# Joining the two attention passes of neighbouring batches on rings of single PSUM banks, in a fused attention, state-space and expert kernel

## The reference

```
qkv    = x @ w_qkv.T + b_qkv                # 16 heads of 16 features
attn   = softmax(q @ k.T / 4)               # 512 x 512 for each head
h      = (attn @ v) @ w_out.T + b_out
h      = concatenate([h, txt], axis=1)      # 589 tokens
u      = layernorm(h);  xp = u @ x_proj.T
delta  = softplus(xp[:, :64] @ dt_proj.T + dt_b)
state  = exp(delta * A) * state + delta * B * u     # 589 steps, 256 features x 16 states
h      = h + sum(state * C) + u * D_skip
h      = h + one_of_14_experts(layernorm(h))
h      = h + causal_attention(layernorm(h))
h      = h + two_of_128_experts(layernorm(h))
```

## Time and profile before

| what | us |
|---|---|
| median of 3 runs | 1209.46 |
| lowest, highest | 1206.95, 1211.32 |
| span of the profiled execution | 1222.6 |
| of it, until the end of the last recurrence | 691 |

### The profile page before, as it was taken

One profiled execution on the slowest core, in us unless ns is written; L12 is line 12 of the kernel. 1 busy time (PEld: TensorE's weight loads), 2 busy tenths in 40 slices (PEclk: granted clock), 3 DMA queues, 4 the chain that ended last, 5 costly groups with the idle time before them and its releaser, 6 DMA issues.

```text
span 1222.6 us, 14392 instructions
## 1 busy us (share of the span) xinstructions
PE 929.1 (76%) x4656; PEld 511.5 (42%) x4657; DVE 763.9 (62%) x1348; ACT 440.4 (36%) x819; POOL 205.3 (17%) x248
## 2 busy tenths in 40 slices
PE   6898989879888688974286529999588887548880
PEld 2323432334323243222253229998356565324440
DVE  4803589996899968999779931111467756732225
ACT  1174138750287501873352203444123331212220
POOL 1000001110011100111000142333000203355550
PEclk9989798976889858796687859999799998769995
DMA  3199206873058730597656436664501400249926
GB/s 100 27 326 330 84 23 160 212 166 100 18 151 206 172 109 1 135 213 159 160 181 211 148 128 192 196 195 149 233 1 46 179 6 14 75 140 398 402 75 253
DMA packets 75259, 185.57 MB, mean 152 GB/s; under 512 B 12010, under 2 KB 48573, under 8 KB 72512
## 3 DMA queue, kind: packets, MB, share of 16 engines
q1 hardware_dynamic: 60800, 148.11, 36.9%
q0 software_dynamic: 14400, 36.71, 13.7%
HBM read 124.88 MB, written 43.69 MB: 138 GB/s over the span
## 4 chain that ended last, share of the span: by engine, by line
PE 35%; DVE 29%; issue 19%; DMA 9%; POOL 3%; ACT 2%; another core or an unknown queue 1%; SPq 1%; POOLq 0%; DVEq 0%; ACTq 0%
DVE hst L1639 8%; PE ps L646 7%; DVE hC L1649 5%; PE ps L1139 5%; DMA bc<-bc_dram 4%; DVE mxn L1588 4%; PE ps L1015 3%; PE ps L623 3%; PE ps L1127 2%; POOL ys_dram L1546 2%; PE ps L1087 2%; DMA yodd<-hC 2%; PE ps L741 2%; DVE Hs L2170 1%; PE ps L633 1%
## 5 line engine op out<-in xcount | busy, mean ns | idle before, releaser
L1588 DVE TENSOR_REDUCE mxn<-ps 128x2 f32<-128x1024 f32 x128 | 150.6, 1220 | 60.3 <-PE ps L646 60.0
L1639 DVE TENSOR_TENSOR_SCAN hst<-dA,dBu 128x1180 f32<-128x1180 f32 x64 | 166.9, 2608 | 3.1 <-ACT dA L1209 2.6
L646 PE MATMUL ps<-Kh,Qh 32*128 32x512 f32 x512 | 122.6, 763 | 25.4 <-DVE mxn L1588 24.6
L1217 ACT ACTIVATE Ph<-ps 128x1024 f32<-128x1024 f32 x128 | 125.2, 1077 | 24.1 <-PE ps L741 23.5
L741 PE MATMUL ps<-Qh,Kh 32*128 32x512 f32 x512 | 111.0, 717 | 5.6 <-ACT Ph L1217 5.4
L1630 DVE TENSOR_TENSOR dBu<-dtu,bc 128x1180 f32<-128x1180 f32 x64 | 88.0, 1380 | 14.7 <-DMA bc<-bc_dram 14.5
L1649 DVE TENSOR_TENSOR hC<-hst,bc 128x1180 f32<-128x1180 f32 x64 | 87.2, 1362 | 9.6 <-DMA yodd<-hC 9.6
L1525 POOL DMA_DIRECT2D yS<-hC x24 | 20.8, 868 | 426.6 <-DVE hC L1649 426.6
L1139 PE MATMUL ps<-ring,xgT 128*64 128x256 f32 x512 | 70.1, 395 | 13.6 <-ACT xgT L1477 9.4
L1906 DVE TENSOR_TENSOR yo<-ps,b2r 128x256 f32<-128x256 f32 x32 | 13.6, 425 | 106.4 <-PE ps L938 106.4
L754 PE MATMUL ps<-Ph,Vh 128*32 128x512 f32 x512 | 73.7, 649 | 7.1 <-ACT OT L1221 4.4
(11 more groups left out here) (263 smaller groups left out, 1443.8 us busy)
## 6 DMA issues: line engine op xcount, KB each, us to landing
bc<-bc_dram SPq DMA_DIRECT2D x64, 590.0 KB, 5.9
ring<-in_we SPq DMA_DIRECT2D x16, 2048.0 KB
W<-in_w SPq DMA_DIRECT2D x46, 512.0 KB, 5.9
yS<-hC POOLq DMA_DIRECT2D x24, 590.0 KB, 7.9
yodd<-hC POOLq DMA_DIRECT2D x24, 590.0 KB, 7.8
xs_dram<-zeros SPq DMA_DIRECT2D x1, 8224.0 KB, 43.8
xg<-xs_dram SPq DMA_DIRECT2D x16, 514.0 KB
ys_dram<-zeros SPq DMA_DIRECT2D x1, 5120.0 KB, 48.3
```

The costliest lines, as they stand in the source:

```text
L646: m = nc.tensor.matmul(ps[:, banks.start + hh % 2, :], Qh[HR * hh:HR * (hh + 1), hg, P * i:P * (i + 1)], Kh[HR * hh:HR * (hh + 1), hg, :], ...
L1217: nc.scalar.activation(Ph[:, n % 2, 2 * g:2 * g + 2, :], ps[:, turned_banks(2 * n + g), :], ACT.Exp, scale=float(HD) ** -0.5).then_inc(act ...
L1588: nc.vector.tensor_reduce(slots32(mxn[:, hg % 2, i, :])[:, 2 * g:2 * g + 2, HD], ps[:, score_banks(b, 2 * (QT * hg + i) + g), :], AX.X, AL ...
L1639: nc.vector.tensor_tensor_scan(hst[:, k % 2, :, :].rearrange("p c t -> p (c t)"), dA[:, k % 2, :, :].rearrange("p c t -> p (c t)"), dBu[:, ...
```

## The change

The order of the first attention and the recurrence is written anew. The first pass of batch b + 1 now runs unit by unit beside the second pass of batch b (`attend_ahead`), six units behind: the second pass of batch `eb` goes with units 10 to 15 of the first pass of `eb` and units 0 to 9 of that of `eb + 1`. The lists are

```diff
+        FIRST_SETS = ((0, 1), (2, 3), (5, 6))
+        A_RING, B_RING = (5, 6, 7), (0, 1, 2)
+        PV, MISC = 3, 4
+        LAG = 6
+        ALONE = NU - LAG
+        TURNED = (2, 3, 0, 1)
+        def score_bank(k):
+            if k < 4 * ALONE:
+                return FIRST_SETS[k // 2 % 3][k % 2]
+            return A_RING[k % 3]
+        def unit_at(eb, n):
+            return (eb, ALONE + n) if n < LAG else (eb + 1, n - LAG)
...
+            def score_head(b, u, h):
+                if i == 0 and h == 0:
+                    pe.wait_ge(act_q, 2 * (HG * b + hg) + 2)
+                if freed_by(k):
+                    pe.wait_ge(dve_max, freed_by(k))
+                return nc.tensor.matmul(ps[:, score_bank(k), :], Qh[HR * h:HR * (h + 1), hg, P * i:P * (i + 1)],
+                                        Kh[HR * h:HR * (h + 1), hg, :], start=True, stop=True)
...
+            def turned_head(b, n, x):
+                h = TURNED[x]
...
+                if k >= len(B_RING):
+                    pe.wait_ge(act_p, k - len(B_RING) + 1)
...
+            def both(b, u, eb, n):
+                for x in range(4):
+                    if u is not None:
+                        score_one(b, u, x)
+                    if n is not None:
+                        turned_head(eb, n, x)
+                if n:
+                    weighted(eb, n - 1)
...
+            def attend_ahead(eb):
+                ab = eb + 1
+                for n in range(NU):
+                    if n == 2:
+                        turn_maxima(eb, 2)
+                    elif n in (4, 8, 12):
+                        project(ab, n // 4 - 1, 0)
+                    elif n in (5, 9, 13):
+                        project(ab, n // 4 - 1, 1)
+                    elif n == 6:
+                        turn_maxima(eb, 3)
+                    elif n in (10, 14):
+                        turn_maxima(ab, n // 4 - 2)
+                    elif eb == 0 and n < 2:
+                        project_v(0, n)
+                    b, u = unit_at(eb, n)
+                    both(b, None if eb == 1 and n < LAG else u, eb, n)
+                weighted(eb, NU - 1)
+
+            def first_chain():
+                project(1, 3, 0)
+                turn_heads(0, range(HG))
+                project(1, 3, 1)
+                both(1, ALONE, 0, None)
+                both(1, ALONE + 1, 0, None)
+                turn_values(0, 0)
+                turn_values(0, 1)
+                both(1, ALONE + 2, 0, None)
+                project_out(0, 0)
+                project_out(0, 1)
+                project_v(1, 0)
+                both(1, ALONE + 3, 0, None)
+                project_v(1, 1)
+                both(1, ALONE + 4, 0, None)
+                turn_tokens(0)
+                both(1, ALONE + 5, 0, None)
+                project_x(0)
+                project_dt(0)
...
@@ DVE
+            def head_maxima(b, u, h):
+                dve.wait_ge(pe_s, k + 1)
+                nc.vector.tensor_reduce(slots32(mxn[:, hg % 2, i, :])[:, h:h + 1, HD], ps[:, score_bank(k):score_bank(k) + 1, :], AX.X, ALU.max,
                                         negate=True).then_inc(dve_max, 1)
...
@@ ACT
-                for g in range(2):
-                    act.wait_ge(pe_st, 2 * k + g + 1)
-                    nc.scalar.activation(Ph[:, n % 2, 2 * g:2 * g + 2, :], ps[:, turned_banks(2 * n + g), :], ACT.Exp, scale=float(HD) ** -0.5).then_inc(act_p, 1)
+                for x in range(4):
+                    act.wait_ge(pe_st, 4 * k + x + 1)
+                    nc.scalar.activation(Ph[:, n % 2, TURNED[x], :], ps[:, B_RING[(4 * k + x) % 3], :], ACT.Exp,
+                                         scale=float(HD) ** -0.5).then_inc(act_p, 1)
```

More of the change, by code:

```diff
@@ L119, in fusion_kernel @@
         dA = eb("dA", [P, 2, KC, LP])
[L120 removed]
+        dBu = eb("dBu", [P, 2, KC, LP])
         hst = eb("hst", [P, 2, KC, LP])
@@ L841, in back_ahead @@
-            def back_ahead(eb, cb):
-                for u in range(NU):
-                    tscores(eb, u)
-                    if u:
-                        weighted(eb, u - 1)
-                weighted(eb, NU - 1)
-                turn_heads(eb, range(HG))
-                for half in range(2):
-                    turn_values(eb, half)
-                for half in range(2):
-                    project_out(eb, half)
-                if eb < NB - 1:
-                    for hg in range(QG):
-                        for which in range(2):
-                            project(eb + 1, hg, which, gap_bank(hg, which))
-                room = low if eb == NB - 1 else tail
-                turn_tokens(eb, room)
-                project_x(eb, room)
-                project_dt(eb, room)
-                if eb == NB - 1:
-                    turn_both(cb)
-                    skip(eb)
+                        at = D * (i - first) + P * c
@@ new lines, in scan_beside_chain @@
+            def scan_beside_chain(cb):
+                eb, ab = cb + 1, cb + 2
+                project(ab, 3, 0)
+                project(ab, 3, 1)
+                turn_heads(eb, range(HG))
+                project_v(ab, 0)
+                project_v(ab, 1)
+                turn_values(eb, 0)
+                turn_values(eb, 1)
+                if cb:
+                    for r in range(len(Y_ROUNDS)):
+                        turn_both(cb - 1, r)
+                project_out(eb, 0)
+                project_out(eb, 1)
+                turn_tokens(eb)
+                project_x(eb)
+                project_dt(eb)
@@ new lines, in scan_beside_attention @@
+            def scan_beside_attention():
+                cb, eb = NB - 2, NB - 1
+                for n in range(NS):
+                    if n == 1:
+                        turn_maxima(eb, 2)
+                    elif n == 2:
+                        turn_maxima(eb, 3)
+                    ahead = remaining(n)
+                    behind = units_ahead(n)
+                    for k in range(max(len(ahead), len(behind))):
+                        both(eb, ahead[k] if k < len(ahead) else None, eb, behind[k] if k < len(behind) else None)
+                    if n == 1:
+                        for r in range(len(Y_ROUNDS)):
+                            turn_both(cb - 1, r)
+                    if n == 9:
+                        weighted(eb, NU - 1)
+                        turn_heads(eb, range(HG))
+                    elif n == 10:
+                        turn_values(eb, 0)
+                        turn_values(eb, 1)
+                    elif n == 11:
+                        project_out(eb, 0)
+                        project_out(eb, 1)
+                    elif n == 13:
+                        turn_tokens(eb)
+                        project_x(eb)
+                    elif n == 14:
+                        project_dt(eb)
```

724 lines of the change are left out of this document (385 added, 339 removed).

## The result

| | median us | lowest to highest |
|---|---|---|
| before, 4 runs | 1210.39 | 1206.95 to 1214.40 |
| changed, 4 runs | 1335.21 | 1314.46 to 1347.85 |

The ratio is 1.093, with a 95% interval of 1.0823 to 1.1037. The forecast was 1272, with 1218 to 1302 as its range. The direction was right, and the median lies 33 us above the range. The profiled span went from 1222.6 to 1331.6 us, +109, where the prediction had +67.

The account below looks back on a forecast made before the run. It took DVE to bound the recurrences and to wait for PE's scores in first passes. +51 us at full clock plus 16 for the clock gave +67 on the span, rounded to 1209.5 + 62 = 1272 us; range 1218 to 1302.

Parts of the forecast that it names:

- The joined step: Four first-pass heads, four second-pass heads and four weighted matmuls, on rings of three banks: 4.0 us at full clock.
- The three joined stretches: First pass of one batch beside second pass of another, for batches 0, 1 and 2: 82 + 80 + 80 us.
- Rival 1: Joined steps: PSUM emptying binds, not the ring; step 2.4 us, total 1183 to 1198 us; chance 0.10.
- Rival 2: Joined steps: PE binds and the ring's wait is hidden; step 3.0 us, total 1212 to 1230; chance 0.17.
- Rival 3: The low clock holds for most of the joined stretches; steps of 6.8 us, total 1310 and more; chance 0.08.
- My allowance of 16 us: Added to the span for stretches at the low clock, between bounds of 0 and 30 us.
- Recurrence 2 with the rest of the third first pass ... 119: Recurrence 2: 93.6 us busy, 24 maxima 14.4, two `minus` 1.3, y 4.6, waits 5; 119 us.
- Recurrences 0 and 1: Two recurrences with `step_size` and `input_size` moved in, and y added in the second: 92.5 and 98 us.
- 6 us once a batch: Possible cost if the transfer of bc, issued in the recurrences and at the chain, came late.
- first_chain: Stretch after the first joined one: PE work 22 us, maxima 15, softplus and fetches 9, delta, `dtu` and decay 4; 50 us.
- The 5 us that I took off the last one for `skip`: Last recurrence: 95.8 us with 8.5 idle, less 5 because `skip` no longer waits for y.
- Start of the first joined stretch: Before batch 0's joined stretch: 42 us plus 7.6 for two projections, half of `project_v` and fetches; 49.6 us.

Follow-up runs that it names:

- e4: Changed kernel with maxima of joined heads, and exponentials of batches 1 and 2, reading 64 columns, matmuls whole: one execution took 1275.42 us.
- e7: Changed kernel with the weighted matmuls issued after the second, third and fourth pair of heads in turn, step by step: 1294.57 us, ratio 1.0828.
- e5: Changed kernel with six single banks instead of three for batch 3's second pass, from its sixth unit on: 1274.95 us, ratio 1.0678.
- e1: Changed kernel with the weighted matmuls issued ahead of the fourth pair of heads in every step: 1295.4 us, ratio 1.0863.
- e8: Kernel before with single heads on six single banks and one-head maxima in batch 0's first pass: 1211.15 us, ratio 1.001.
- e9: Kernel before with one-head maxima in all first passes, six single banks in batch 0, four in batches 1 to 3: 1212.36 us, ratio 1.0007.
- e10: Kernel before with second passes on a ring of three single banks and exponentials of one bank, old order: 1412.67 us, ratio 1.1685.
- c_after: The changed kernel run again, unaltered, beside the second group of experiments: median 1307.08 us, ratio 1.0912 to the kernel before.

## Why the prediction was right in direction and too small

- **The joined step: right.** 3.96 us against 4.0, with both waves where they were put. e4 confirms the mechanism behind it. The three joined stretches sum to 240.0 us against 242.
- **Rival 1 (emptying binds): refuted.** DVE is busy for 43.6 of 79.4 us and its maxima wait 139.6 us for scores in the whole span.
- **Rival 2 (PE binds at 3.0): refuted.** No regular step is that short. The single steps of 2.91 us in e7 show that PE could do it.
- **Rival 3 (low clock in the joined stretches): wrong place.** They stood at 1.00, 0.91 and 0.96. My allowance of 16 us was laid there too; no such sum was needed there, and more than that fell due in the recurrences.
- **The step that failed is the term "Recurrence 2 with the rest of the third first pass ... 119".** It added up DVE's work and 5 us of waits. The work was near (108.1 us busy against 114), but DVE stood idle for 53 us, 37.9 of them before scans whose decays were late. I had priced the needed row myself, a step of the second pass alone at 4.0 us, and 6.8 at the low clock, but set it only against the joined stretches. Laid against the states it would have shown the bound: 16 steps over nine states are 7.1 us a state at full clock and 12.1 at the low one (6.8 x 16/9), against 5.1 us of DVE in a state without maxima. ACT takes its list in order, so decays stand behind exponentials that wait for PE, and PE's fourth head waits for the ring. e5 removes this wait by three more banks: 29 to 32 us less, 0.5 us of the wait left, and 110.9 us scan to scan, against 101.9 before. At full clock three banks cost 7.9 us of such waits (e1, in its own order), so the larger part of the miss is the ring together with the low clock in this stretch (0.62), for which the sum had nothing either.
- **Recurrences 0 and 1: 13 us too short.** In recurrence 0 DVE waits 5.6 us for the rows of B and C, 2.4 for an accumulating DMA and 2.0 for decays. The first comes in seven waits of at most 1.3 us, and 2.3 us of such waits stood in this recurrence before; it is not the one late transfer that I named at "6 us once a batch". DVE's own work grew by 4.0 us, where I had 2.8.
- **`first_chain` and the last recurrence:** 4.3 and 5.7 us too short, the first at a granted clock of 0.74. The 5 us that I took off the last one for `skip` did not come: it lasts 96.5 us, 95.8 before.
- **Start of the first joined stretch, layers behind:** within 3 us. (For the start I wrote 7.6 us; the terms that I list give 3 x 1.98 + 3 x 0.8 = 8.3.) The durations of single-bank instructions were within 1%. e8 and e9 confirm that the single-head maxima are free.
- **The sum:** 61 us more until the end of the last recurrence, of which 42.5 in recurrence 2, minus 16 of clock allowance and 3 in the layers behind, is the 42 between +67 and +109. The other 21 us between the forecast of 1272 and the median of 1335 are no step of the kernel: I took 17.6 off the forecast span of 1289.6 because the profiled execution before lay above its median, and the one after lies 3.6 below.

What stays open: why the clock stays up for longer in recurrence 2 in some kernels than in others (in e1 it stood at 1.00 from 582 to 645 us, with steps of 3.86 from 599 on), which makes up part of the gains of e1 and e7 and, most likely, of the spread of 33 us between runs of the changed kernel. In e5 the longer time at full clock (0.81 against 0.69) and the shorter step come together, and how its gain divides between them is not shown; six banks at the low clock were not seen for long. None of the joined versions tried came near the kernel before: e5, the best of the joined versions that do the whole work, is 6.8% above it. A joined order with more than three banks for each pass wasn't tried; two rings of three with the two other banks use all eight.

## What to carry to other kernels

When a buffer ring is made smaller, price the round trip (producer, consumer, release) for every stretch that uses the ring, also where the work was formerly hidden: beside another engine's loop, compare steps of the round trip per turn of the loop with the loop's own time. An in-order engine that serves both the ring and the loop (ACT here) passes the ring's wait on to the loop. Before moving instructions to fill a wait, count how many slots the ring gives in a round trip: with three slots in 1.9 us and four heads a step, the two other orders tried (e1, e7) moved the wait and left the joined stretches longer than before. And price the trip at the low clock too: here a wait of 2.6 us a state became 8.2.

## What the runs showed of the hardware

The second pass alone on three banks ran for long at the low clock although PE was busy most of the time. In e10 the granted clock was 0.50 (the 1.2 GHz level) in all of 61 to 118 us, with PE busy for 51.14 of these 57.00 us; in the kernel before the same pass stood at 0.88. The ring doesn't fix the level, though: the same pass on the same three banks stood at 1.00 from 590 to 609 us in `c_after` and at 0.50 from 627 to 654, and at 1.00 from 596 to 640 in e1. The joined steps had rings of three and the same wait, and stood at 1.00 for 79.4 us in the first joined stretch and at 0.91 and 0.96 in the others. What differs there is that two heads, one of each pass, run side by side; which property of it counts, no run tells. The Trainium skill, "TensorE: Matmul & The Clock Gate", section "A second HAM failure mode: psum-queue depth-cycling", tells of a kernel in which cycling through PSUM banks leaves small idle times between groups of matmuls, so that the clock gate goes back and forth. The trace of `c_after` agrees in that both levels occur under one ring; in e10 the clock didn't go back and forth in the stretch above: it stayed at 0.50. The joined stretches, which cycle through banks too, show that the cycling isn't enough by itself.
